# Full attention by single score banks: a new order of one step in a fused two-layer transformer kernel

## The reference

```
def xattn1(q, k, v, mask, W_q, b_q, W_k, b_k, W_v, b_v, W_o, b_o):
    qh, kh, vh = proj(q, W_q, b_q), proj(k, W_k, b_k), proj(v, W_v, b_v)   # 16 heads of 16
    scores = jnp.einsum('bhqd,bhkd->bhqk', qh, kh) / jnp.sqrt(16.0)
    scores = jnp.where(mask[:, None, None, :] == 0, -1e9, scores)
    attn = jax.nn.softmax(scores, axis=-1)
    context = jnp.einsum('bhqk,bhkd->bhqd', attn, vh)
    return context.transpose(0, 2, 1, 3).reshape(16, 512, 256) @ W_o.T + b_o
```

## Time and profile before

| | |
|---|---|
| median of 3 runs | 5576.17 us (5572.05 to 5576.94) |
| profiled execution, span from the first to the last instruction | 5563.0 us |
| TensorE busy | 4885.3 us (88%) |
| VectorE busy | 3922.8 us (71%) |
| ScalarE busy | 2689.4 us (48%) |
| GpSimd busy | 951.8 us (17%) |

### The profile page before, as it was taken

One profiled execution on the slowest core, in us unless ns is written; L12 is line 12 of the kernel. 1 busy time (PEld: TensorE's weight loads), 2 busy tenths in 40 slices (PEclk: granted clock), 3 DMA queues, 4 the chain that ended last, 5 costly groups with the idle time before them and its releaser, 6 DMA issues. The chain is left out here.

```text
span 5563.0 us, 90361 instructions
## 1 busy us (share of the span) xinstructions
PE 4885.3 (88%) x28783; PEld 2797.5 (50%) x28784; DVE 3922.8 (71%) x7706; ACT 2689.4 (48%) x3563; POOL 951.8 (17%) x722
## 2 busy tenths in 40 slices
PE   8979988996799999999999999999979119999970
PEld 4546656783344444444444344444337118888860
DVE  7766756655588888887888788888848217777753
ACT  2335542222266767776776677777641004344430
POOL 5620002214400001010000101010003440000016
PEclk9989999998799999999999999999978559999985
DMA  7666644216723233333323332332316331121225
GB/s 226 214 181 162 164 132 117 77 57 189 199 58 70 53 74 72 66 50 63 71 53 73 73 60 48 70 73 42 53 48 193 120 123 61 57 85 54 64 81 187
DMA packets 340005, 544.40 MB, mean 98 GB/s; under 512 B 50785, under 2 KB 251968, under 8 KB 337393
## 3 DMA queue, kind: packets, MB, share of 16 engines
q1 hardware_dynamic: 321456, 487.62, 35.4%
q0 software_dynamic: 14768, 50.51, 2.6%
q10 hardware_dynamic: 3360, 0.98, 0.1%
HBM read 271.54 MB, written 187.80 MB: 83 GB/s over the span
## 5 line engine op out<-in xcount | busy, mean ns | idle before, releaser
L1175 DVE TENSOR_REDUCE full_peak<-full_item 128x1 f32<-128x512 f32 (+2 forms) x3392 | 2036.4, 655 | 462.9 <-PE full_item L1242 457.3
L1145 ACT ACTIVATE full_prob<-full_score 128x1024 f32<-128x1024 f32 (+1 forms) x1792 | 1650.1, 960 | 641.6 <-PE full_score L1253 635.5
L1242 PE MATMUL full_item<-full_kst,full_qst 49*128 49x512 f32 (+1 forms) x4096 | 1204.3, 406 | 35.8 <-DVE full_peak L1175 23.9
L1253 PE MATMUL full_score<-full_qst,full_kst 51*128 51x512 f32 (+1 forms) x3328 | 1109.8, 448 | 20.9 <-ACT full_prob L1145 11.9
L1253 PEld LDWEIGHTS full_score<-full_qst,full_kst 51*128 51x128 f32 (+1 forms) x3328 | 480.1, 183 | 934.3 <-ACT full_prob L1145 599.5
L1267 PE MATMUL full_value<-full_prob,full_vaug 128*17 128x512 f32 x6656 | 886.9, 605 | 0.8 <-ACT full_raw L1132 0.7
L1242 PEld LDWEIGHTS full_item<-full_kst,full_qst 49*128 49x128 f32 x4096 | 630.1, 189 | 180.1 <-DVE full_peak L1175 130.2
L2505 ACT ACTIVATE moe_h<-moe_hbank,moe_b 128x512 f32<-128x512 f32 (+1 forms) x320 | 199.6, 624 | 460.5 <-PE moe_hbank L2598 457.0
L2608 PE MATMUL moe_ybank<-moe_w_both,moe_h_high 128*128 128x512 f32 x1088 | 389.2, 400 | 0.0
L744 DVE TENSOR_REDUCE win_peak<-win_item 128x2 f32<-128x384 f32 x512 | 262.0, 553 | 123.9 <-PE win_item L784 117.2
L718 ACT ACTIVATE win_prob<-win_score 128x768 f32<-128x768 f32 x256 | 207.4, 811 | 266.6 <-PE win_score L798 222.5
(11 more groups left out here) (272 smaller groups left out, 6969.3 us busy)
## 6 DMA issues: line engine op xcount, KB each, us to landing
full_kst<-full_high SPq DMA_DIRECT2D x256, 200.1 KB
full_ctxT<-in_ctxT SPq DMA_DIRECT2D x16, 1601.0 KB, 8.8
full_kst<-full_low SPq DMA_DIRECT2D x128, 200.1 KB
win_qst<-scratch_q SPq DMA_DIRECT2D x384, 64.0 KB, 2.8
full_qst<-scratch_q SPq DMA_DIRECT2D x384, 64.0 KB
scratch_xbuf<-ctxp_zero POOLq DMA_DIRECT2D x17, 1024.0 KB, 8.1
scratch_attn<-win_raw SPq DMA_DIRECT2D x64, 256.0 KB, 2.1
scratch_q<-open_parts SPq DMA_DIRECT2D x64, 256.0 KB, 3.8
```

The source lines that it names most:

```text
L1145: nc.scalar.activation(prob[h][(s.par * PAIRS + t) % 2][0:rows, 0:banks, :], score[u % 2][0:rows, 0:banks, :], ACT.Exp, scale=SCALE).then_ ...
L1175: nc.vector.tensor_reduce(peak[s.par][:, hq:hq + len(qts), c], src, AX, ALU.max).then_inc(item_read, 1)
L1242: ins = nc.tensor.matmul(ps[:, at:at + z - a], qst[s.slot][rows, h // 2, qt * P:(qt + 1) * P].bitcast(F32R), kst[s.slot][rows, h // 2, a:z ...
L1253: ins = nc.tensor.matmul(score[u % 2][0:z - a, kt % 2, :], kst[s.slot][rows, h // 2, a:z].bitcast(F32R), qst[s.slot][rows, h // 2, :].bitc ...
```

## The change

Four single score banks take the place of two double ones. A unit is one key tile of one head, the order of the scores is key tile by key tile over the four heads, and each exp reads 512 columns. Each score matmul signals and waits for the exp four units back. `prob` has four buffers of one tile for each head, the products of a key tile wait for its own four exps and signal each time. The order of a step is one string (`STEP_ORDER`), and the half of each item comes from a second one (`ITEM_HALVES`). ACT copies the previous step's values behind its fifth exp instead of its fourth. POOL makes `high` itself, as a copy rounded to fp32r, in one instruction; DVE's four parts go.

```diff
-    SCORES = [(t, h, kt) for t in range(PAIRS) for h in range(GROUP) for kt in range(2 * t, min(2 * t + 2, KT))]
+    SCORE_BANKS = 4
+    PROB_BUFS = 4
+    SCORES = [(h, kt) for kt in range(KT) for h in range(GROUP)]
...
-    JOBS_AFTER = (6, 8, 16, 18)
-    VALUES_AFTER = (4, 10, 14, 20, 24, 28, 32, 38, 41, 44, 48, 50, 52)
-    ITEMS_AFTER = (1, 0, 1, 0, 1, 2, 1, 2, 3, 0, 1, 0, 1, 1, 1, 2, 1, 2, 3, 0, 1, 0, 1, 1, 1, 0,
-                   1, 1, 1, 0, 1, 1, 1, 2, 1, 0, 1, 0, 1, 2, 0, 0, 1, 2, 1, 0, 1, 2, 2, 1, 2, 2)
-    HIGH_PARTS = 4
-    HIGH_AT = (6, 12, 18, 24)
+    STEP_ORDER = ("SSSIJSSSIIIVIISISVISSSIISVISSSIIJISISISJISSSIIVSIISSIVSISISSIVSIIISSISISJIIISSSSIVIISSSIVISISSIVSSSI"
+                  "SIIVIISIISVSIIISVSIIVII")
+    ITEM_HALVES = ("100111011010101011001011011010111111110101111110110110")
+    READ_VALUES_AT = 4
...
-        score = [ps(f"score{i}", [P, 2, 512]) for i in range(2)]
+        score = [ps(f"score{i}", [P, 512]) for i in range(SCORE_BANKS)]
...
-        high = [sb(f"high{c}", [P, SK]) for c in range(KC)]
+        high = [sb(f"high{c}", [P, SK], F32R) for c in range(KC)]
...
-        prob = [[sb(f"prob{h}{i}", [P, 2, SQ]) for i in range(2)] for h in range(GROUP)]
+        prob = [[sb(f"prob{h}{i}", [P, SQ]) for i in range(PROB_BUFS)] for h in range(GROUP)]
...
             def low_of(b, c):
-                pool.wait_ge(high_done, HIGH_PARTS * (KC * b + c + 1))
-                nc.gpsimd.tensor_tensor(low[c][:, :], low[c][:, :], high[c][:, :], ALU.subtract).then_inc(low_done, 1)
+                pool.wait_ge(kept_done, KC * b + c + 1)
+                pool.sem_inc(high_start, 1)
+                nc.gpsimd.tensor_copy(high[c][:, :], low[c][:, :]).then_inc(high_done, 1)
+                pool.wait_ge(high_done, KC * b + c + 1)
+                nc.gpsimd.tensor_tensor(low[c][:, :], low[c][:, :], high[c][:, :].bitcast(F32), ALU.subtract).then_inc(low_done, 1)
...
-                    at_least(act, value_done, PAIRS * s.n + t - 1)
-                    rows, banks = (P, 2) if KT > 2 * t + 1 else (K_LAST, 1)
-                    nc.scalar.activation(prob[h][(s.par * PAIRS + t) % 2][0:rows, 0:banks, :],
-                                         score[u % 2][0:rows, 0:banks, :], ACT.Exp, scale=SCALE).then_inc(score_read, 1)
-                    if e == 3 and not first:
+                    at_least(act, value_done, KT * s.n + kt - PROB_BUFS + 1)
+                    nc.scalar.activation(prob_of(s, h, kt)[0:rows, :], score[score_bank(u)][0:rows, :], ACT.Exp,
+                                         scale=SCALE).then_inc(score_read, 1)
+                    if e == READ_VALUES_AT and not first:
                         read_values(s.plus(-1))
...
-            def high_of(b, c, part):
-                lo, hi = part * SK // HIGH_PARTS, (part + 1) * SK // HIGH_PARTS
-                dve.wait_ge(kept_done, KC * b + c + 1)
-                nc.vector.tensor_scalar(high[c][:, lo:hi].bitcast(U32), low[c][:, lo:hi].bitcast(U32), HIGH_BITS, None,
-                                        ALU.bitwise_and).then_inc(high_done, 1)
...
-            def scores(s, u, t, h, kt):
-                if kt % 2 == 0:
-                    at_least(pe, score_read, first_unit(s) + u - 1)
+            def scores(s, u, h, kt):
+                at_least(pe, score_read, first_unit(s) + u - SCORE_BANKS + 1)
...
-                if kt % 2 == 0:
-                    pe.wait_ge(score_read, unit(s, "exp", GROUP * (kt // 2) + GROUP - 1) + 1)
+                pe.wait_ge(score_read, unit(s, "exp", GROUP * kt + GROUP - 1) + 1)
...
-                if kt == KT - 1 or kt % 2 == 1:
-                    ins.then_inc(value_done, 1)
+                ins.then_inc(value_done, 1)
```

More of the change, by code:

```diff
@@ L873, in units @@
     def units(s):
[L875 to L880, removed]
+        given, jobs = iter(range(EXPS)), iter(range(4))
+        out = [("exp", next(given)) if t == "S" else ("job", next(jobs)) for t in STEP_ORDER if t in "SJ"]
+        return [u for u in out if busy(s) or u[0] == "exp"]
     def first_unit(s):
@@ L893, in other_halves @@
     def other_halves():
[L895 to L898, removed]
+        out = [int(c) for c in ITEM_HALVES]
         out.pop(NMAX - HEAD + AHEAD)
@@ L949, in batch_par, with score_bank @@
         return s.turn % 2 if isinstance(s.turn, int) else s.k // 4 % 2
+    def score_bank(u):
+        return (len(ALL_JOBS) + u) % SCORE_BANKS
+    assert UNITS % SCORE_BANKS == 0 and EXPS % SCORE_BANKS == 0
     with ExitStack() as ctx:
@@ L1036, in load @@
                     rows = slice(64 * (s.slot % 2) + 32 * half_row, 64 * (s.slot % 2) + 32 * half_row + 32)
-                    for at, part in ((0, high), (HD, low), (2 * HD, high)):
-                        sp.dma_start(k[m + at:m + at + HD, :, :], part[c][rows, :]).then_inc(into, 16)
+                    for at, part in ((0, high[c][rows, :].bitcast(F32)), (HD, low[c][rows, :]), (2 * HD, high[c][rows, :].bitcast(F32))):
+                        sp.dma_start(k[m + at:m + at + HD, :, :], part).then_inc(into, 16)
             def send_shift(s):
@@ L1107, in _, with read_job @@
             act.wait_ge(ones_set, 2)
-            def read_job(number, par, what, b, vpar):
+            def read_job(number, at, what, b, vpar):
                 kind, a, j = what
                 act.wait_ge(score_full, number + 1)
-                bank = score[number % 2 if isinstance(number, int) else par][:, 0, :]
+                bank = score[number % SCORE_BANKS if isinstance(number, int) else at]
                 if kind == "K":
@@ L1193, in window @@
             def window(s, first, left):
-                for n, it in enumerate(window_items(s, left)):
-                    if n in HIGH_AT and s.slot % 2 == 1 and busy(s):
-                        high_of(s.turn + 1, s.slot // 2, HIGH_AT.index(n))
+                for it in window_items(s, left):
                     item(*it)
@@ L1205, in _, with job @@
                 ins = nc.tensor.matmul(value[:, i * P:(i + 1) * P], shift_parts[:, :], ident[:, :], start=True, stop=True)
-            def job(number, par, what, b, cpar):
+            def job(number, at, what, b, cpar):
                 kind, a, j = what
-                at_least(pe, score_read, number - 1)
-                bank = score[number % 2 if isinstance(number, int) else par][:, 0, :]
+                at_least(pe, score_read, number - SCORE_BANKS + 1)
+                bank = score[number % SCORE_BANKS if isinstance(number, int) else at]
                 if kind == "K":
@@ L1281, in window @@
                 pe.wait_ge(shift_in[s.slot], 32 * (s.turn + 1))
[L1282 to L1291, removed]
-                            item(*it)
[L1293 to L1300, removed]
+                u = given = group = 0
+                for token in STEP_ORDER:
+                    if token == "S":
+                        scores(s, u, *SCORES[units(s)[u][1]])
+                        u += 1
+                    elif token == "J" and busy(s):
+                        job(first_unit(s) + u, score_bank(u), JOBS[s.slot][units(s)[u][1]], s.turn + 1, 1 - batch_par(s))
+                        u += 1
+                    elif token == "I":
+                        for it in items[given:given + 1]:
+                            item(*it)
+                        given += 1
+                    elif token == "V":
+                        if group > 0:
+                            values(s, group - 1)
+                        elif not first:
+                            values(s.plus(-1), KT - 1)
+                        group += 1
             windows_by_batch(pe, window)
```

27 lines of the change are left out of this document (12 added, 15 removed).

## The result

The changed kernel takes 5450.0 us (median of 4 runs, 5441.95 to 5453.82) against 5576.3 (4 runs, 5572.05 to 5576.94) of the kernel before beside it: ratio 0.9774, 95% interval 0.976 to 0.9788. The forecast was 5455. Its profiled execution has a span of 5449.8 us, 113 less than before.

What follows compares the result with a forecast made beforehand. TensorE bounds the kernel, held 3.3 us a step by ScalarE and VectorE. Per step -3.3 + 0.7 (floor) + 0.65 (waiting left), rounded to 1.9 gained; 64 steps give 122, less 1 at the start: 5455 us, range 5422 to 5530.

Steps and rivals of the forecast that it cites:

- The stretch arithmetic: TensorE, scores and maxima between full-array pieces: 0.89 us for three matmuls in the fuller half, 0.24 for each more.
- The floor of 37.8: TensorE's time for a key-job step when nothing holds it: 37.8 us in the new order, 37.1 in the old.
- The stalls: TensorE held by ScalarE and VectorE in each attention step: 3.3 us before, 0.65 after, bounds 0 and 3.3.
- the walk: Both orders stepped through by rules from the trace: 3.4 us of waiting a step in the old, 0.3 to 0.9 new.
- In the steps: nothing: GpSimd making the keys' high part costs attention steps nothing; only the start comes 1.1 to 2.2 us later, 1 taken.
- The length of that copy: GpSimd's copy of 1601 columns for the high part: 2.5 to 3.6 us each.
- The exps: ScalarE's single-tile exps: 0.59 us long, 0.49 apart, some 1.5 us more a step, covered by its idle time.
- The value copy: ScalarE's copy of the previous step's values, before key tile 0's products: 1.73 against 1.87 us on TensorE, hidden by 0.14.
- Handovers: Rival, 15%: extra signals and waits in each step give back part of the gain, 0.8 us a step; 5510 us.
- DVE sets the pace: Mechanism of the 9% stalls-stay rival: VectorE's reductions keep the 3.3 us of waiting, uneven halves add 0.7; 5621 us.
- Even: Rival, 6%: the kernel comes out even, with waiting staying at 2.4 to 2.8 us a step.
- The signs of being wrong: Exps over 0.55 apart, products awaiting the value copy, maxima awaiting VectorE over 1 us a step, costlier matmuls, longer loop-turn pause.

Runs made afterwards that it cites:

- the last experiment: GpSimd's copy made to wait until the step's shift is split, against the changed kernel, run a second time: 5412.3 us, 0.9708 of the kernel before.

## Why the prediction was right, and where it erred

**The stretch arithmetic held.** A V is still 0.98 (2387.57 to 2388.55), a stretch of three 0.89, of four 1.13 or 1.14 (1.03 where one of the four is the second half of a four-part maximum, which the prediction counts as two). The two stretches of six took 1.83 (2375.87 to 2377.70, with two maxima of two parts in it) and 1.70; 1.6 was forecast. In return the stretch of five, which has a four-part maximum in it, took 1.26, not 1.37, and that of the transpose 1.39 (2388.55 to 2389.94), not 1.58. The floor of 37.8 for a step with key jobs, worked out from the old trace, is the measured 37.75 of the last experiment. With the other jobs in place of the key jobs (four of 1.92 for the long value step, 1.3 more) it gives 39.1, and 38.96 was measured, so the floor is good to some 0.15.

**The stalls: more of them removed than forecast.** The term was 3.3 of waiting before and 0.65 after. With the copy out of the shift's way, steps stand at their floor, and halving the reductions takes no more than 0.2 off them, so the waiting that the order leaves is 0 to 0.2; the walk was some 0.5 too pessimistic. From 160.7 to 150.9 for four steps is 2.45 a step, against 1.95 forecast. The single banks alone give 0.6 of this, and the order without them loses: neither part brings the gain by itself. What in the order does it is argued by the walk and not shown. The reason given there, at most five scores between two full-array pieces, can't be all of it: the old string breaks that only once, with six in one stretch, and has at most four in every other.

**The step that failed: "In the steps: nothing" for GpSimd's copy.** It was costed by POOL's own idle time, and what the copy might do to an operation of DVE was put at nothing without a reason. POOL's time was indeed free, but its copy held one short operation of DVE for 1.05 us in 30 steps, right where the next items wait, and PE came 0.9 later. That is 30 x 0.9 = 27 us; the experiments put the whole at 31 to 36 (5450.0, 5447.8 against 5416.9, 5412.3), and the 4 to 9 beyond that are no more than what two profiles of the changed kernel differ by (2415.4 and 2405.1 us for the 63 steps), in single long steps at a lower granted clock. Nor does the hold come with the move alone: on the kernel before, the same copy met no `tensor_scalar`; it takes the new order's timing as well. So 5455 was met by two errors of opposite sign: 0.5 a step too little for the order (32 us), 0.45 a step not charged to GpSimd's part (28 us). That the sum was right to 5 us is luck; its terms were right only to 30.

**The length of that copy** is 1.52 us, not 2.5 to 3.6. The nearest rows were a 256-column copy and a subtraction; the first scaled by columns carried a fixed part with it (400 columns took 0.52 in the run with four pieces, 1601 take 1.52). Nothing came of it but the start: all is 0.8 later there, 1 forecast.

**The exps.** 0.60 long and 0.49 to 0.50 apart, as the short ones of 65 partitions promised; ACT is busy 29.99 in the step, 29.9 forecast. The timeline of ACT:

```profile
2356.14 1.57 ACT L1151 ACTIVATE full_prob<-full_score 128x512 f32<-128x512 f32 x3 [1.38 <-PE full_score L1247]
2358.22 0.59 ACT L1129 COPY full_vaug<-full_score 128x512 f32<-128x512 f32 x1 [0.50 <-PE full_score L1219]
```

Three in 1.57 are two distances of 0.49 and one length.

**The value copy** was called hidden by 0.14. PE waited for it once in the run (0.3 us; its weight loads 15.4 in all, under other matmuls), and three exps later it is not hidden and costs 192 us. Three exps at 0.49 are 1.47, and PE stood 1.36: by that estimate the margin was about 0.1, so the forecast's 0.14 was about right.

**The rivals.** *Handovers*: refuted here, by 39 extra signals a step that cost nothing, by steps that meet a floor with no such term in it, and by exps that follow at 0.49. *DVE sets the pace*: as a reason for a slower kernel, refuted; half reductions showed that DVE's pace is worth 0.2 a step, not 3.3. Yet its sign was good: the loss that there is does come through DVE, by way of the held shift. *Even*: not so.

**The signs of being wrong.** One of them did appear: the loads of maxima wait 7 us a step for DVE by name (452.3 / 64), where over 1 was to mean trouble. But only the 0.9 of the key-job steps reached PE's time; the sum of waits by name, which the prediction itself didn't want to subtract, was a poor sign. The pause where the loop turns over is about as long as it was: PE stands 4.06 and 5.41 us there, and 4.37 and 5.06 in the second profile, against 4.44 and 4.24 before.

**The row and the rule.** The forecast went by the pace in the row (0.24 from signal to signal) and not by the semaphore tail of the Trainium skill, "TensorE: Matmul & The Clock Gate", Part 3. Here the trace decides for the row: PE waits for none of the 39 extra signals, and they change no step by more than 0.02 us.

## What to carry to other kernels

- When an operation moves from DVE to GpSimd, its cost is not only GpSimd's time: list what short operation of DVE can fall into it and what waits behind that one. Whether it does fall into it hangs on the order of the rest: the same copy met nothing in the old order. A wait that puts the long copy behind the short operation gave 31 to 36 us; cutting the copy in four gave 20.
- A median over a group hides such a loss: L1182 has a median of 175 ns and a maximum of 1266. Look at the maximum and at every second step, not at one window. The window that I show above happened to be an undisturbed one.
- Write a step's floor as stretches between the pieces that use the whole array and compare every kind of step with it. Where a step lies 0.9 above the floor that the others meet, there is a cause to be found.

## What the runs showed of the hardware

- A DVE `tensor_scalar` of 16 columns took 174 ns alone and up to 1266 ns when a GpSimd cast of 1.52 us had begun before it, up to 3575 ns behind a GpSimd subtraction of 3.6 us, and with casts of a quarter of the columns at most 257 ns; it ended 0.03 us behind the GpSimd instruction each time. A `tensor_reduce` in the same place kept its 0.22 us.
- GpSimd casts 128x1601 fp32 to fp32r in 1.52 us; its subtraction of the same size takes 3.62.
- With pauses of 1.4 us once in a step of 40 us the granted clock fell from 1.00 to between 0.87 and 0.96 in some windows of 40 us, unevenly from step to step, and the kernel lost more than the pauses: 192 us, where they are 87 together.
- In the last four steps of the stage the granted clock differed between profiles of the same kernel (0.83 and 0.90, 0.86 and 0.91), and where it was lower these steps took 6 to 9 us more.
- 39 more semaphore increments by matmuls in 38 us changed no step by more than 0.02 us.
